# Selective-scan layer: the last one or two states of each half-stage leave the transposes and are summed in channel layout on GpSimd and VectorE

## The reference, cut to what matters

```python
xc = silu(conv(x))                                  # 1024 channels x 1024 positions per batch
dt = softplus(dt_r @ dt_proj + dt_bias)
for n in range(16):                                 # the states
    h_n = exp(dt * A_n) * h_n(previous) + dt * xc * B_n   # a scan over the positions
    y  += h_n * C_n                                 # C_n: one number per position
y = (y + D * xc) * silu(z)
s = y @ out_proj.T
g = silu(down(silu(gate(xn)) * up(xn)))
out = x + s * g
```

## Time and profile before

| | |
|---|---|
| median of 3 runs | 1173.33 us (1170.23 to 1177.11) |
| the profiled execution's own time | 1170.76 us |
| its span in the trace | 1168.9 us |
| TensorE busy | 1114.6 us, 95% of the span |
| VectorE busy | 947.9 us, 81% |
| GpSimd busy | 734.4 us, 63% |
| ScalarE busy | 644.6 us, 55% |
| transposes of states (L944) | 2048 instructions, 281.7 us busy |
| GpSimd's products (L594) | 256, mean 2570 ns |
| scans (L1189) | 256, mean 2279 ns |

### The profile page before, as it was taken

The page is one execution under the profiler, slowest core; times in us unless marked ns, Lnnn a source line. Parts: engine busy times, 40 slices in busy tenths (PEclk is TensorE's granted clock), DMA queues, the critical chain, the costliest instruction groups (busy, mean ns, idle before and its releaser), DMA issues.

```text
span 1168.9 us, 12511 instructions
## 1 busy us (share of the span) xinstructions
PE 1114.6 (95%) x4430; PEld 595.2 (51%) x4430; DVE 947.9 (81%) x789; ACT 644.6 (55%) x816; POOL 734.4 (63%) x406
## 2 busy tenths in 40 slices
PE   5998999999999999999999899999999999999998
PEld 3443455555545555555444345555555555555543
DVE  4897899999789999985325379999988899999630
ACT  3225577777717777760022357777874477787200
POOL 2000899999537999980410048999973599999211
PEclk9998999999999999999999999999999999999999
DMA  8663389999914999988511125999994289999841
GB/s 252 207 219 115 105 204 222 216 246 239 247 49 125 226 225 223 250 179 285 200 36 36 45 78 147 218 232 223 240 226 143 102 191 231 207 256 213 251 175 45
DMA packets 61778, 214.26 MB, mean 183 GB/s; under 512 B 6666, under 2 KB 6794, under 8 KB 61204
## 3 DMA queue, kind: packets, MB, share of 16 engines
q0 software_dynamic: 16128, 88.09, 38.4%
q1 hardware_dynamic: 44004, 119.70, 30.6%
q10 hardware_dynamic: 1584, 5.68, 1.2%
HBM read 102.52 MB, written 22.85 MB: 107 GB/s over the span
## 4 chain that ended last, share of the span: by engine, by line
PE 48%; POOL 24%; DVE 14%; issue 8%; DMA 3%; ACT 2%; POOLq 0%; DVEq 0%; SPq 0%; ACTq 0%
POOL ub L594 20%; PE psM L966 11%; PE psM L1026 9%; PE psA L806 9%; DVE hb L1189 8%; PE psT L944 7%; PE psM L956 4%; POOL yT L604 4%; PE psM L836 4%; DVE xc L1053 2%; DMA yT<-yc 2%; PE psA L916 1%; DVE hid L1053 1%; DMA w_ts<-w_in_dram 1%; PE psM L860 1%
## 5 line engine op out<-in xcount | busy, mean ns | idle before, releaser
L594 POOL TENSOR_TENSOR ub<-dtx,bn 128x1024 f32<-128x1024 f32 x256 | 645.8, 2570 | 287.8 <-DMA bn<-ss_rows_scratch 187.5
L1189 DVE TENSOR_TENSOR_SCAN hb<-psA,ub 128x1024 f32<-128x1024 f32 x256 | 579.7, 2279 | 10.6 <-POOL ub L594 4.8
L699 ACT ACTIVATE psA<-dt,cc 128x1024 f32<-128x1024 f32 x256 | 285.9, 1118 | 129.4 <-DVE hb L1189 128.7
L836 PE MATMUL psM<-xnT,w_ts 128*126 128x512 f32 x704 | 329.0, 598 | 4.4 <-DVE th L1053 4.2
L944 PEld LDWEIGHTS psT<-ident,hb 128*128 128x128 f32 x2048 | 233.4, 140 | 179.0 <-issue 87.1
L944 PE MATMUL psT<-ident,hb 128*128 128x128 f32 x2048 | 281.7, 276 | 16.7 <-DVE yT L1053 14.8
L720 ACT ACTIVATE yc<-psT,ssm 128x512 f32<-128x512 f32 x336 | 217.4, 678 | 51.4 <-PE psT L944 49.2
L836 PEld LDWEIGHTS psM<-xnT,w_ts 128*126 128x126 f32 x704 | 122.5, 190 | 113.0 <-issue 113.0
L966 PE MATMUL psM<-w_dn,hid 126*128 126x512 f32 x352 | 164.3, 594 | 0.0
L1053 DVE SCALAR_TENSOR_TENSOR yT<-psT,ssm,yT 128x512 f32<-128x512 f32 x144 | 104.9, 735 | 31.6 <-PE psT L944 30.3
L956 PE MATMUL psM<-xnT,w_ts 128*128 128x512 f32 x256 | 119.6, 594 | 2.2 <-DMA w_ts<-w_in_dram 2.2
(11 more groups left out here) (82 smaller groups left out, 530.3 us busy)
## 6 DMA issues: line engine op xcount, KB each, us to landing
yT<-yc POOLq DMA_DIRECT2D x112, 768.0 KB, 8.8
bn<-ss_rows_scratch SPq DMA_DIRECT2D x64, 512.0 KB, 7.0
w_ts<-w_gu_scratch SPq DMA_DIRECT2D x44, 504.0 KB, 4.7
w_ts<-w_in_dram SPq DMA_DIRECT2D x32, 256.0 KB, 7.2
hb<-z_scratch SPq DMA_DIRECT2D x16, 512.0 KB, 8.0
w_gu_scratch<-hid ACTq DMA_DIRECT2D x11, 504.0 KB, 4.2
yT<-x_dram SPq DMA_DIRECT2D x8, 512.0 KB, 9.0
z_scratch<-th SPq DMA_DIRECT2D x16, 256.0 KB, 8.1
```

The source lines that it names most:

```text
L594: pool.tensor_tensor(ub[:, i % 2, :], dtx[:, i, :], bn[:, t, :], ALU.mult).then_inc(s_u, 1)
L699: act.activation(psA[:, i % 2, :], dt[:, i, :], ACT.Exp, scale=negA[:, h * DH + i, bass.ds(n, 1)]).then_inc(s_a, 1)
L836: mm = pe.matmul(psM[0:IM, gu, :], w_ts[:, t, at:at + IM], xnT[:, k, h * CH:(h + 1) * CH], start=(k == 0), stop=(k == HK - 1))
L1189: dve.tensor_tensor_scan(hb[:, t * DH + i, :], psA[:, i % 2, :], ub[:, i % 2, :], 0.0, ALU.mult, ALU.add).then_inc(s_scan, 1)
```

## The change

States from `ROWS[h]` on are not turned: state 15 in the first half-stage of a batch, 14 and 15 in the second.

- For these states SP loads the row of C, broadcast over the partitions, into `bn` (new step "C"). In the second half-stage, C's row 14 goes into slot 0 when B's row 14 has been used, and C's row 15 into slot 1 when B's row 15 has been used for all four blocks. In the first half-stage C's row 15 goes into slot 0. To have the rows in HBM, B's and C's rows are turned and stored together (32 rows in place of 16).
- GpSimd multiplies the four blocks of state 15 in place by C's row (`times_c` of GpSimd), after its last `input`. In the second half-stage VectorE multiplies those of state 14 (`times_c` of VectorE), one in each quarter of state 14, between the scans of state 15.
- VectorE adds: in the quarters of state 15 `add_skip` (now `D*xc` plus the product), in the second half-stage also `add_last` (plus the other product). `add_skip` does not wait for `turn_back` any more; what follows `turn_back` is `add_rows`, a plain addition of `psT`.
- `add_y`, `scale_y`, `turn` and the gathers of the left-out states are gone. `turn_back` waits for the gathers itself.
- While states are turned TensorE does 2 steps per quarter; what is left is spread over the quarters without turning (14 over 4, or 28 over 8).
- z comes back into `xnT` in the second half-stage. "C" stands behind ("B", 15); ("d", 1, 0) stands behind "back". The next half-stage's first B row waits for GpSimd's `times_c`.

```diff
+ROWS = [NS - 1, NS - 2]
+STEP = 2
 def steps_of(p, h):
     steps = STEPS if h else STEPS[:-REST]
-    return steps[len(steps) * p // QUARTERS:len(steps) * (p + 1) // QUARTERS]
+    turned = 4 * (ROWS[h] - LATE)
+    if p < turned:
+        return steps[STEP * p:STEP * (p + 1)]
+    left, at, n = len(steps) - STEP * turned, p - turned, QUARTERS - turned
+    return steps[STEP * turned + left * at // n:STEP * turned + left * (at + 1) // n]
...
-           ("B", 14), ("z", 3, 1), ("G", 0), ("w",), ("B", 15), ("d", 0, 0), ("d", 1, 0), ("W",), ("N", 0), ("back",),
-           ("G", 1),
-           ("d", 2, 0), ("N", 1), ("d", 3, 0)]
+           ("B", 14), ("z", 3, 1), ("G", 0), ("w",), ("B", 15), ("C",), ("d", 0, 0), ("W",), ("back",), ("d", 1, 0),
+           ("N", 0), ("G", 1), ("d", 2, 0), ("N", 1), ("d", 3, 0)]
...
+                        elif what[0] == "C":
+                            for n in range(ROWS[h], NS):
+                                t = n - ROWS[h]
+                                sp.wait_ge(s_u, unit(b, h, NS - 1 + t, 0) + 8)
+                                sp.dma_start(bn[:, t, :], ss_rows[b, R + NS + n:R + NS + n + 1, :].to_broadcast([P, L])).then_inc(s_crow[t], 16)
...
-                    gather_y(NS - 2, 1)
+                    def times_c(i):
+                        pool.wait_ge(s_scan, unit(b, h, NS - 1, i) + 3)
+                        pool.tensor_tensor(hb[:, DH + i, :], hb[:, DH + i, :], bn[:, h, :], ALU.mult).then_inc(s_hc, 1)
+                    pool.wait_ge(s_crow[h], 16 * (b + 1) if h else 16 * (b * HALVES + 1))
+                    for i in range(DH):
+                        if h == 0 and i == DH - 1:
+                            gather_y(ROWS[0] - 1, 1)
+                        times_c(i)
...
                     def add_skip(i):
+                        k, m = blk(b, h, i), h * DH + i
+                        if h == 0:
+                            dve.wait_ge(s_hc, k + 1)
+                            stt(xc[:, m, :], xc[:, m, :], cc[:, m, DP:DP + 1], hb[:, DH + i, :], ALU.mult,
+                                ALU.add).then_inc(s_ym, 1)
+                        else:
+                            dve.wait_ge(s_hc1, b * DH + i + 1)
+                            stt(xc[:, m, :], xc[:, m, :], cc[:, m, DP:DP + 1], hb[:, i, :], ALU.mult,
+                                ALU.add).then_inc(s_ym1, 1)
+                    def times_c(i):
+                        dve.wait_ge(s_crow[0], 16 * (b * HALVES + 2))
+                        dve.wait_ge(s_scan, unit(b, h, NS - 2, i) + 3)
+                        dve.tensor_tensor(hb[:, i, :], hb[:, i, :], bn[:, 0, :], ALU.mult).then_inc(s_hc1, 1)
+                    def add_last(i):
+                        k, m = blk(b, h, i), h * DH + i
+                        dve.wait_ge(s_hc, k + 1)
+                        dve.wait_ge(s_ym1, b * DH + i + 1)
+                        dve.tensor_tensor(xc[:, m, :], xc[:, m, :], hb[:, DH + i, :], ALU.add).then_inc(s_ym, 1)
+                    def add_rows(i):
                         k, m = blk(b, h - 1, i), (h - 1) * DH + i
                         dve.wait_ge(s_yb, k + 1)
-                        stt(xc[:, m, :], xc[:, m, :], cc[:, m, DP:DP + 1], psT_row, ALU.mult, ALU.add).then_inc(s_ybr, 1)
+                        dve.wait_ge(s_ym, k + 1)
+                        dve.tensor_tensor(xc[:, m, :], xc[:, m, :], psT_row, ALU.add).then_inc(s_ybr, 1)
...
                         if p == 0:
                             hidden(IT - 1, (IT - 1) % 2)
+                        if h and n == NS - 2:
+                            times_c(q)
+                        if n == NS - 1:
+                            add_skip(q)
+                        if h and n == NS - 1:
+                            add_last(q)
                         if h + 1 < HALVES and n == NS - 1 and q > 0:
                             drive(h + 1, q - 1)
```

More of the change, by code:

```diff
@@ L103, with y_pos, rows_ahead @@
 Y_ORDER = [2, 0, 3, 4, 5, 1, 6, 7]
[L106 to L115, removed]
+def y_pos(tb):
+    return Y_ORDER.index(tb)
+def rows_ahead(b, h):
+    return b * sum(ROWS) + sum(ROWS[:h])
 SCRATCH = 2048
@@ L283, in build @@
         s_ybr = sem("s_ybr")
+        s_crow = [sem("s_crow0"), sem("s_crow1")]
+        s_hc = sem("s_hc")
+        s_hc1 = sem("s_hc1")
+        s_ym1 = sem("s_ym1")
+        s_ym = sem("s_ym")
         s_zl = [sem(f"s_zl{i}") for i in range(DH)]
@@ L479, in load_b @@
                         sp.wait_ge(s_u, unit(b, h, n, 0) + 4)
+                        if n == 0 and h:
+                            sp.wait_ge(s_hc, blk(b, h, 0))
+                        elif n == 0 and b:
+                            sp.wait_ge(s_hc1, b * DH)
+                        elif n == 1 and h == 0 and b:
+                            sp.wait_ge(s_hc, blk(b, h, 0))
                         sp.dma_start(bn[:, t, :], ss_rows[b, bass.ds(n + R, 1), :].to_broadcast([P, L])).then_inc(s_B[t], 16)
@@ L773, in _ @@
                             for tb in Y_ORDER[2 * i:2 * i + 2]:
-                                if not by_dve(n, tb):
+                                if not by_dve(tb):
                                     scale_y(n, tb)
@@ L785, in _ @@
                         for tb in Y_ORDER[2 * (p % 4):2 * (p % 4) + 2]:
-                            if not by_dve(LATE + p // 4, tb):
+                            if LATE + p // 4 < ROWS[h] and not by_dve(tb):
                                 scale_y(LATE + p // 4, tb)
@@ L922, in turn_back @@
                         pe.wait_ge(s_tdve, summed(b, h, 0, 0))
+                        for e in range(2):
+                            pe.wait_ge(s_yacc[e], gathered(b, h - 1, ROWS[h - 1] - 1))
                         pe.wait_ge(s_ybr, blk(b, h - 1, i) + 1)
@@ L1184, in scan @@
                             dve.wait_ge(s_y, blk(b, h - 1, i) + 2)
+                        if h and n == 1:
+                            dve.wait_ge(s_ym, blk(b, h - 1, i) + 1)
                         dve.wait_ge(s_a, unit(b, h, n, i) + 1)
@@ L1234, in _ @@
                         for i in range(DH):
-                            add_skip(i)
+                            add_rows(i)
                             times_z(i)
@@ L1256, in _ @@
                     else:
-                        add_skip(0)
+                        add_rows(0)
                         times_z(0)
                         drive(1, 3)
-                        add_skip(1)
+                        add_rows(1)
                         scan(0, 0, 0)
                         times_z(1)
-                        add_skip(2)
+                        add_rows(2)
                         silu_late(0, "d", JD - 1, 0)
@@ L1266, in _ @@
                         times_z(2)
-                        add_skip(3)
+                        add_rows(3)
                         silu_gate(0, 0)
```

64 lines of the change are left out of this document (33 added, 31 removed).

## The result

The changed kernel takes 1198.53 us (median of 4 runs, 1197.33 to 1200.45) against 1172.98 for the kernel before beside it (4 runs, 1170.23 to 1177.11): a ratio of 1.022 [1.0194, 1.0247], slower by 1.9 to 2.5%. The forecast was 1184.0 and the range ended at 1195. The profiled execution took 1200.45 us, its span is 1198.6, 29.7 more than before.

What follows compares the result with a forecast made beforehand. It took scans to pace the early states and TensorE the last dozen us of a half-stage. Sum: 1170.8 + 15.2 (second half-stages, 2 x (5.6 + 2.0)) - 2.0 (first ones) = 1184.0 us; range 1166 to 1195.

Steps and rivals of the forecast that it cites:

- +5.6: End of a second half-stage: GpSimd's products and VectorE's two-SBUF operations exclude each other, ending at 547.0 against 541.3 before.
- Rival 1: VectorE and GpSimd do not get into each other's way; second half-stages 2 x -2.2, total 1164 us; chance 0.15.
- +2.0: Behind TensorE's gap in a second half-stage: the granted clock falls, 3 to 5 us of half speed; between 0 and 3.4.
- twice 7.6 = 15.2: Both second half-stages per kernel: 2 x (5.6 + 2.0) us, for mutual exclusion and the clock's fall.
- The gate as no separate cost: Gate g: store later by the same 5.5 us, load used just when block 2's projection wanted it; no extra cost.
- 500.96 + 10.4: TensorE, second half-stage: scan 13's end plus turning it and 8 steps, given as up to 511.7.
- First half-stages ... -2.0 for both together, between -4.5 and +4: First half-stages: half of the 2.5 and 1.3 us gains at turn_back was taken, giving -2.0 for both.
- up to 2.3: Start of the next half-stage: GpSimd's first two products meet times_z(0), costing it up to 2.3; slack before scan(0, 0).
- The gain at `turn_back`: First half-stages: turn_back 2.5 us earlier in the first batch, 1.3 in the second, as TensorE's lag shrinks.
- Rival 4: Everything in series: C's rows 3 us later, times_c waits for each u, first half-stages lose 2 each; 1195; chance 0.12.
- Rival 3: TensorE is the bound throughout: 192 transposes fewer make it 21 us less, 1150; chance 0.03.
- The chance of 0.67 for slower: Whole kernel: chance 0.67 that it measures slower by more than about 0.5%, 6 us.

Runs made afterwards that it cites:

- experiment 4: Changed kernel with VectorE's add_skip and add_last of the second half-stages reading their last operand from PSUM instead of hb (output incomplete): 1180.16 us, ratio 1.0057.
- experiment 3: Changed kernel without GpSimd's products by C's rows (semaphores still incremented, rows still loaded; output lacks factor C in state 15): 1175.86 us, ratio 1.001.
- experiment 5: Changed kernel with eight useless TensorE matmuls behind the first part of the projection, in the gap before the second turn_back: 1191.08 us, ratio 1.0134.
- experiment 12: Changed kernel with only state 15 unturned, B's row 15 first, hand-spread steps, GpSimd's products waiting for last drive, last gather one product earlier: 1173.62 us, ratio 1.0012.
- experiment 1: Changed kernel with B's row 15 loaded ahead of ("G", 0) and ("w",) in SP's late order: 1191.65 us, ratio 1.0152.
- Experiment 9: The kernel of experiment 1, with GpSimd's products 1 to 3 of state 0 in second half-stages waiting for VectorE's last drive: 1187.8 us, ratio 1.0129.
- experiment 2: Changed kernel with the steps spread evenly over all 32 late quarters again, as before the change: 1198.13 us, ratio 1.0197.

## Why the prediction was right and where it failed

**Right: the second half-stages.** The forecast's steps can be read off, with the 5.8 us taken away by which the half-stage starts late. GpSimd's products start at 526.2 (forecast 526.8). The first `turn_back` is at 536.9 (535.8). `add_rows(0)` begins at 545.6 and ends at 546.8 (547.0). The gap is 7.30 us (some 8). Up to the second `turn_back` a second half-stage is 5.4 and 5.7 us longer than before. So the +5.6 stands, and its cause, taking turns, is shown by experiment 4. The lengths add up as turns: four products at 2.3 and the three VectorE operations that end among them at 1.2 make 12.8, and GpSimd's block takes 12.69. Rival 1 is out. By experiments 3 and 4 the half-stage without exclusion is 1.1 to 1.9 us shorter than before, close to the -2.2 of rival 1, so that rival was right about the price of its own case.

**Nearly right: the clock.** The term +2.0 for "3 to 5 us of half speed" measured 2.3 and 2.8 (experiment 5), for 4.6 and 5.8 us. The twice 7.6 = 15.2 measured 17.2: 11.1 of turns, 5.1 of clock, and 0.9 of a longer low clock at the input projection, whose length varies by itself. The gate as no separate cost held in the changed kernel, where nothing waits for its load; it did not in experiment 12. Two sums in the forecast are off by little: 500.96 + 10.4 is 511.4 and not 511.7, and 547.0 less 541.3 is 5.7.

**Failed: "First half-stages ... -2.0 for both together, between -4.5 and +4".** It measured +12.3, and its place in the sum takes the result out of the range. `turn_back` was to come 2.5 and 1.3 us earlier and came 3.7 and 3.9 later. Three pieces:

- *B's row 15*, 4.2 + 3.1 = 7.3 us (experiment 1). The forecast followed the new spread on TensorE, where it does take the wait for z's weights away: none stands there in the trace after. It did not follow it on SP: the last z store comes later with the steps, SP waits for it in front of ("G", 0), and row 15 is behind. The prediction checked SP's queue for the steps it moves ("C", ("d", 1, 0)), not for the dues that the new spread moves.
- *GpSimd's first two products against `times_z(0)` and `drive(3)`*, 2.8 + 3.7 = 6.5 us: so much longer than before is the stretch from `turn_back` to the next first scan in experiment 1. Experiment 9 takes 1.3 + 2.1 = 3.4 of it away; the other 1.5 + 1.7 = 3.2 go with `times_z(0)`, which its wait does not free, and that they are the collision's is read from the trace (1.6 and 1.8 us over 1.2), not tested. The forecast named this collision, "up to 2.3", and laid it to the slack before scan(0, 0). There is no such slack: in the trace of experiment 1 VectorE goes from `drive(3)` through `add_rows` to the scan without idling, so a late `drive` is a late scan.
- *The gain at `turn_back`*, -1.4 - 0.1 = -1.5 us. With the row on time `turn_back` is 198.9 us behind the first scan in batch 0 (before 200.3) and 199.1 in batch 1 (before 199.2): half of the 2.5 hoped for, and next to nothing of the 1.3. VectorE's work behind it is what the stage then ends with. 7.3 + 6.5 - 1.5 make the 12.3.

**The rivals.** Rival 4 (1195) comes nearest in number, and two of its three reasons are wrong: C's row was on time within 0.6 us, and VectorE's eight `times_c` take 1.19 to 1.42 us each with no idle time before them; that the first half-stages lose more than gain was right. Rival 3 fell: TensorE's share of the chain halved with 192 transposes gone. The chance of 0.67 for slower fits.

**What stays open.** Why experiment 2's last half-stage alone waits for z's weights while the same place in batch 0 does not, no run tells. Experiment 3 has first half-stages 11.0 us longer than before and second ones 3.7 shorter, by the traces. Its own trace shows the same two causes as the changed kernel's: GpSimd waits 3.20 us for B's row 15, the scan 2.96, the clock is low for 3.4 us from 299.2, and `turn_back` is 3.4 and 4.0 us late; behind it `drive(2)` takes 3.38 and `times_z(0)` 2.06 beside GpSimd's first two products, and 1.8 us are lost in each batch. The two cures were not run together with it.

## What to carry to other kernels

Before work is moved to "idle" engines, count which of their operations read two SBUF tiles, since on GpSimd and VectorE these run in turns: what looked like 9 us on one engine beside 9 on the other was 18 in a row; an operand in PSUM, or all of it on one engine, was quicker here. When the spread of independent steps over a stage is changed, follow every store that a step makes due through the in-order DMA queue, to the next load behind it. And a kernel whose engine on the critical path gets a hole of 7 us pays for the hole and again for the clock behind it (here 2.3 and 2.8 us). Matmuls without use in the hole gave that back; useful work moved into it was not tried here.

## What the runs showed of the hardware

Two engines that exclude each other do not always take turns one by one. In the second half-stage they did (rows above). In a first half-stage VectorE's `add_skip(0)` stood through several of GpSimd's instructions. GpSimd, then VectorE, changed kernel:

```profile
305.19 7.46 POOL L641 TENSOR_TENSOR hb<-hb,bn 128x1024 f32<-128x1024 f32 x3
312.12 1.36 POOL L626 DMA_DIRECT2D yT<-yc  x1
312.73 3.13 POOL L641 TENSOR_TENSOR hb<-hb,bn 128x1024 f32<-128x1024 f32 x1
```

```profile
308.49 9.66 DVE L1087 SCALAR_TENSOR_TENSOR xc<-xc,cc,hb 128x1024 f32<-128x1024 f32 x2
318.07 1.21 DVE L1201 TENSOR_TENSOR dtx<-dt,xc 128x1024 f32<-128x1024 f32 x1
```

The second row holds two instructions: the first began at 308.49 and took 8.46 us for its 1.2 us of work, until GpSimd's last product was through. It was so in both batches. It cost nothing, since TensorE had its steps till `turn_back`: without the products (experiment 3) `turn_back` is 203.6 us behind the first scan, with them 203.9. Why GpSimd gave way between its products in the one place and not in the other, no run here tells.
